# Moving the layer norm's centring from GpSimd to ScalarE in the second attention phase of a four-layer cross-attention kernel

## The chip, the cores and the metric

The kernel runs on one core of one Trainium2 chip. The metric is the device time of one execution in microseconds (us). The engines are named as the profile names them: PE is TensorE, PEld its weight loads, DVE is VectorE, ACT is ScalarE, POOL is GpSimd, SP issues DMAs.

## The reference

Four layers follow each other on x of shape 64 x 128 x 128 (batch, tokens, features), with a context of 77 keys per batch and 16 heads of 8 features. The change is in the second layer, L1, whose end is a residual sum and a layer norm:

```
scores = einsum(q, k) / sqrt(d) * attention_weights
scores = where(attention_mask, -inf, scores)
p_attn = softmax(scores);  out = (p_attn @ v) @ Wo.T + bo
x = queries + out
mu = mean(x, axis=-1);  var = mean(square(x - mu), axis=-1)
return (x - mu) * rsqrt(var + 1e-5) * gamma + beta
```

## The kernel before

The program runs seven phases one after the other: A0, F0, A1, A2, F2, A3, F3. A phases are attention, F phases feed-forward. Only A1 (layer L1) is touched. A phase handles 64 batches in a software pipeline: in step b every engine works on several batches at once, its program being one `step` function per engine in a fixed order, unrolled four times inside a loop. Engines meet only through semaphores, which the code calls events. The tiles of the norm have two slots, used in turn by even and odd batches.

In A1, step b, the engines do this, in this order:

- **DVE** (`step_weighted`): scores times weights for batch b+1 (`weigh`, two halves, L856); `variance(b-3)` (L927, adds epsilon to the variance); `mask(b+1, 0)` (L861, mask tile times a large negative number plus the scores, both in SBUF); `invert` (L896); `peak_masked(b+1, 0)` (L869, row maxima); `normalise`, `keep_v`, `sums(b-2)` (L915); `mask(b+1, 1)` (L861); `statistics(b-2)`; `peak_masked(b+1, 1)` (L869); `aggregate(b-2)` (L923, makes mean and variance).
- **POOL**: `shift(b, 1)` (L989, subtract the row maximum, needs the second peak); `root(b-3)` (L1004, power -1/2 on 128x1); `residual(b-1)` (L995); `centre(b-3)` (L1008, (t - mean) * rstd, 128x128); `shift(b+1, 0)` (L989, needs the first peak of b+1); `affine(b-3)` (L1013 times gamma, L1016 plus beta).
- **ACT**: `keep_att(b-1)` (L799), `keep_oT` (L805), `exps(b, 1)` (L747, needs `shift(b, 1)`), `keep_pT(b, 0)` (L752), `block_keys(b+2)` (four L767), `keep_q` (L786), `keep_xT(b+3)` (L774), `keep_pT(b, 1)` (L752), `exps(b+1, 0)` (L747, needs `shift(b+1, 0)`).
- **PE**: scores of b+1 (L646, needs `block_keys` and `keep_q`), the attention products of b-1 (L681), transposes of the probabilities (L664), the projections (L618 to L707).

`peak_masked(b, k)` also waits until `shift(b-1, k)` has read the maxima, and `sums(b)` until the z of batch b-2 is made. In phases A0 and A2 the POOL program is another branch: `rstd` (L999 adds epsilon on POOL, then `root`), `residual`, `centre`, `block_keys`, `affine`.

Of the kernel before, what the change touches and what calls it, by code (L numbers as in the profile page):

```python
# [138 lines left out]
def build_layers(nc, a, out):  # L139
# [3 lines left out]
    with ExitStack() as ctx:  # L143
# [3 lines left out]
        def slots(name, shape, dt=F32, n=2):  # L147
            return [sb(f"{name}{s}", shape, dt) for s in range(n)]
# [140 lines left out]
        mv_s = slots("mv", [T, 2])  # L289
        var_s = slots("var", [T, 1])  # L290
        rstd_s = slots("rstd", [T, 1])
        z_s = slots("z", [T, D])
        zg_s = slots("zg", [T, D])
        y_s = slots("y", [T, D])
# [77 lines left out]
        def event(name, phases, parts=1, transfers=0):  # L372
            return Event(sem, name, [(ph, NB if ph[0] == "A" else GROUPS) for ph in phases], parts, transfers)
# [37 lines left out]
        mv_made = event("mv_made", CROSS)  # L411
        var_made = event("var_made", CROSS)
        rstd_made = event("rstd_made", CROSS)
        z_made = event("z_made", CROSS)
        zg_made = event("zg_made", CROSS)
        y_made = event("y_made", CROSS)
# [325 lines left out]
        def cross_scalar(act, ph):  # L742
            w = cross[ph]

            def exps(b, k):
                act.wait_ge(shifted.sem(b), shifted.count(ph, b, k))
                nc.scalar.activation(half(p_s[b.par], k), half(p_s[b.par], k), ACT.Exp, scale=SCALE[ph]).then_inc(exp_made.sem(b), 1)  # L747

            def keep_pT(b, k):
                act.wait_ge(pT_made.sem(b), pT_made.count(ph, b, k))  # L750
                wait_earlier(act, att_made, ph, b, 1, k)
                nc.scalar.activation(pT_s[k][:], two[0:C, :], ACT.Copy).then_inc(pT_kept.sem(b), 1)  # L752

            def keep_k(b):
                act.wait_ge(k_made.sem(b), k_made.count(ph, b))
                wait_earlier(act, kblk_made, ph, b, 2)
                src = k_col_bank[:, K_COL:K_COL + C]
                if ph == "A2":
                    nc.scalar.activation(kT_s[b.par][:], src, ACT.Copy).then_inc(k_kept.sem(b), 1)
                else:  # L760
                    nc.scalar.activation(kT_s[b.par][:], src, ACT.Identity, bias=w["bk"][:, 0:1]).then_inc(k_kept.sem(b), 1)

            def block_keys(b):
                act.wait_ge(k_made.sem(b), k_made.count(ph, b))
                wait_earlier(act, s_made, ph, b, 2)
                for h in range(QH):
                    ins = nc.scalar.activation(kblk_s[b.par][:, h * C:(h + 1) * C], k_col_bank[:, K_COL:K_COL + C], ACT.Identity,  # L767
                                               bias=key_bias_rows[:, h:h + 1], scale=rowmask[:, h:h + 1])
                ins.then_inc(kblk_made.sem(b), 1)

            def keep_xT(b):
                act.wait_ge(xT_made.sem(b), xT_made.count(ph, b))
                wait_earlier(act, q_made, ph, b, 2)
                nc.scalar.activation(xT_s[b.par][:], att_bank[:, X_COL:X_COL + T], ACT.Copy).then_inc(xT_kept.sem(b), 1)  # L774

            def keep_q(b, columns):
                act.wait_ge(q_made.sem(b), q_made.count(ph, b))

                if columns:
                    act.wait_ge(xT_made.sem(columns), xT_made.count(ph, columns))  # L780
                wait_earlier(act, s_made, ph, b, 2)
                src = att_bank[:, Q_COL:Q_COL + T]
                if ph == "A2":
                    nc.scalar.activation(qT_s[b.par][:], src, ACT.Copy).then_inc(q_kept.sem(b), 1)
                else:
                    nc.scalar.activation(qT_s[b.par][:], src, ACT.Identity, bias=w["bq"][:, 0:1]).then_inc(q_kept.sem(b), 1)  # L786

            def keep_v(b):
                act.wait_ge(v_made.sem(b), v_made.count(ph, b))
                wait_earlier(act, att_made, ph, b, 2, 1)  # L790
                dst = v_s[b.par][:].rearrange("p (h v) -> p h v", v=VPAIR // 2)[:, :, 0:DH]
                src = v_bank[0:C, V_COL:V_COL + D].rearrange("p (h v) -> p h v", v=DH)
                nc.scalar.activation(dst, src, ACT.Copy).then_inc(v_kept.sem(b), 1)

            def keep_att(b):
                act.wait_ge(att_made.sem(b), att_made.count(ph, b, 1))

                wait_earlier(act, back_made, ph, b, 2)
                nc.scalar.activation(att_s[b.par][:], att_bank[:, 0:2 * T], ACT.Copy).then_inc(att_kept.sem(b), 1)  # L799

            def keep_oT(b):
                act.wait_ge(oT_made.sem(b), oT_made.count(ph, b))
                if (b + -2).exists:
                    act.wait_ge(proj_made.sem(b + -2), proj_made.count(ph, b + -2))
                nc.scalar.activation(oT_s[b.par][:], out_bank[:, OT_COL:OT_COL + T], ACT.Copy).then_inc(oT_kept.sem(b), 1)  # L805

            def step(b, has):
                weighted = ph == "A1"
                if has(-1):
                    keep_att(b + -1)  # L810
                if has(-2) and ph != "A0":
                    keep_oT(b + -2)
                if has(0) and weighted:
                    exps(b, 1)
                if has(0):
                    keep_pT(b, 0)
                if has(2):
                    block_keys(b + 2) if weighted else keep_k(b + 2)
                if has(1) and not weighted:
                    keep_v(b + 1)  # L820
                if has(2):
                    keep_q(b + 2, b + 3 if has(3) else None)
                if has(3):
                    keep_xT(b + 3)
                if has(1) and not weighted:
                    exps(b + 1, 0)
                if has(0):
                    keep_pT(b, 1)
                if has(1):
                    exps(b + 1, 0 if weighted else 1)  # L830
            drive(act, NB, step, reach=REACH)

        def cross_vector(dve, ph):
# [88 lines left out]
            def aggregate(b):  # L922
                nc.vector.bn_aggr(mv_s[b.par][:], stats_s[b.par][:]).then_inc(mv_made.sem(b), 1)  # L923

            def variance(b):
                dve.wait_ge(mv_made.sem(b), mv_made.count(ph, b))
                nc.vector.tensor_scalar(var_s[b.par][:], mv_s[b.par][:, 1:2], LN_EPS, None, ALU.add).then_inc(var_made.sem(b), 1)  # L927

            def step_weighted(b, has):
                if has(1):  # L930
                    weigh(b + 1, 0)
                    weigh(b + 1, 1)
                if has(-3):
                    variance(b + -3)
                if has(1):
                    mask(b + 1, 0)
                if has(-1):
                    invert(b + -1)
                if has(1):
                    peak_masked(b + 1, 0)  # L940
                if has(-1):
                    normalise(b + -1)
                if has(1):
                    keep_v(b + 1)
                if has(-2):
                    sums(b + -2)
                if has(1):
                    mask(b + 1, 1)
                if has(-2):
                    statistics(b + -2)  # L950
                if has(1):
                    peak_masked(b + 1, 1)
                if has(-2):
                    aggregate(b + -2)
# [23 lines left out]
        def cross_gpsimd(pool, ph):  # L978
# [18 lines left out]
            def rstd(b):  # L997
                pool.wait_ge(mv_made.sem(b), mv_made.count(ph, b))
                nc.gpsimd.tensor_tensor(var_s[b.par][:], mv_s[b.par][:, 1:2], ln_eps[:, 0:1], ALU.add).then_inc(var_made.sem(b), 1)  # L999
                root(b)  # L1000

            def root(b):
                pool.wait_ge(var_made.sem(b), var_made.count(ph, b))
                nc.gpsimd.tensor_tensor(rstd_s[b.par][:], var_s[b.par][:], minus_half[:, 0:1], ALU.pow).then_inc(rstd_made.sem(b), 1)  # L1004
                pool.wait_ge(rstd_made.sem(b), rstd_made.count(ph, b))

            def centre(b):
                nc.gpsimd.tensor_scalar(z_s[b.par][:], t_s[b.par][:], mv_s[b.par][:, 0:1], rstd_s[b.par][:, 0:1],  # L1008
                                        ALU.subtract, ALU.mult).then_inc(z_made.sem(b), 1)

            def affine(b):
                pool.wait_ge(z_made.sem(b), z_made.count(ph, b))
# [5 lines left out]
            def step(b, has):  # L1018
                weighted = ph == "A1"
                if weighted:  # L1020
                    if has(0):
                        shift(b, 1)
                    if has(-3):
                        root(b + -3)
                    if has(-1):
                        residual(b + -1)
                    if has(-3):
                        centre(b + -3)
                    if has(1):
                        shift(b + 1, 0)  # L1030
                    if has(-3):
# [1006 lines left out]
```

## Time and profile before

| | us |
|---|---|
| median of 3 runs | 2476.26 |
| range of the runs | 2475.57 to 2477.04 |
| the profiled execution's own time | 2477.04 |
| its span in the trace | 2475.2 |

Over the whole span the profile has PE busy 93%, DVE 76%, POOL 63%, ACT 60%; A1 lies between about 523 and 930 us. Starts in the trace are in us from the span's start; a row's second number is its duration, and what stands in brackets at its end is how long the engine was idle before it and who ended that. Consecutive instructions of one engine overlap by some hundredths of a microsecond in these rows. A duration includes time in which an issued instruction is held up inside its engine.

### The profile page before, as it was taken

What the parts mean: (1) busy time and instruction counts of PE and PEld (TensorE: products, weight loads), DVE (VectorE), ACT (ScalarE), POOL (GpSimd) and SP (SyncE); (2) the same over time, 40 slices, a digit from 0 to 9 for tenths busy, and PEclk for the clock granted to TensorE, in tenths of its full rate; (3) what the DMA queues carried; (4) which work ended last, traced back from release to release, by engine and by line L of the source; (5) the groups of instructions that cost most, each with busy time, mean ns of one, the idle gap of its engine ahead of it and who ended that gap; (6) DMA issues with size and microseconds to landing.
All of it is one profiled execution on the core that took longest, in us unless ns stands there. A gap on an engine that the chain in (4) does not pass through costs nothing.

```text
span 2475.2 us, 83166 instructions
## 1 busy us (share of the span) xinstructions
PE 2305.7 (93%) x26926; PEld 1818.4 (73%) x26926; DVE 1877.8 (76%) x4067; ACT 1476.8 (60%) x3343; POOL 1560.6 (63%) x2374
## 2 busy tenths in 40 slices
PE   6999998988888879999999979999999999999899
PEld 4777777966666667777777867777777777777587
DVE  4777772159999985777775668888888888888566
ACT  4777775558888875888884524444444444444333
POOL 2666663139999992666666766666666666666332
PEclk9999999989999997999999989999999999999999
DMA  4111111245555541222221223333333333333111
GB/s 125 43 43 42 43 41 57 69 134 165 169 166 169 166 116 40 52 51 52 50 48 56 70 71 96 92 96 97 96 95 94 94 94 94 94 94 92 48 56 55
DMA packets 443043, 211.78 MB, mean 86 GB/s; under 512 B 206400, under 2 KB 433856, under 8 KB 442816
## 3 DMA queue, kind: packets, MB, share of 16 engines
q1 hardware_dynamic: 442944, 210.51, 32.1%
q8 instruction: 56, 0.92, 0.2%
q14 instruction: 43, 0.35, 0.0%
HBM read 113.36 MB, written 29.88 MB: 58 GB/s over the span
## 4 chain that ended last, share of the span: by engine, by line
PE 64%; POOL 13%; issue 8%; SPq 5%; ACT 4%; DVE 3%; DMA 2%; POOLq 0%; DVEq 0%; ACTq 0%
PE bank L664 10%; PE bank L1429 8%; PE bank L1389 8%; PE bank L681 5%; PE bank L1126 5%; PE bank L646 4%; PE bank L1457 4%; POOL sb_region L989 4%; PE bank L1140 4%; ACT sb_pT L752 3%; PE bank L1439 3%; PE bank L1415 3%; POOL sb_rstd L1004 2%; SPq L1334 2%; POOL sb_z L1008 2%
## 5 line engine op out<-in xcount | busy, mean ns | idle before, releaser
L664 PE MATMUL bank<-sb_ident,sb_region 128*77 128x128 f32 x3072 | 413.1, 278 | 54.1 <-ACT sb_pT L752 50.5
L752 ACT ACTIVATE sb_pT<-bank 77x1024 f32<-77x1024 f32 x384 | 392.2, 1021 | 82.7 <-PE bank L664 81.9
L664 PEld LDWEIGHTS bank<-sb_ident,sb_region 128*77 128x77 f32 x3072 | 350.0, 151 | 108.2 <-issue 104.3
L1519 ACT ACTIVATE sb_l<-sb_l 128x640 f32<-128x640 f32 x128 | 94.4, 738 | 384.3 <-DVE sb_l L1567 384.3
L843 DVE TENSOR_REDUCE sb_max<-bank 128x8 f32<-128x616 f32 x256 | 203.1, 793 | 149.0 <-PE bank L646 80.4
L747 ACT ACTIVATE sb_region<-sb_region 128x616 f32<-128x616 f32 x384 | 276.8, 721 | 22.9 <-POOL sb_region L989 21.5
L1640 POOL TENSOR_TENSOR sb_pn<-sb_l,sb_r_all 128x512 f32<-128x512 f32 x128 | 134.6, 1052 | 231.9 <-DVE sb_r_all L1577 227.8
L1389 PE MATMUL bank<-sb_region,sb_wqkv 128*128 128x128 f32 x2048 | 253.7, 278 | 1.5 <-DVE sb_region L1555 0.8
L1429 PE MATMUL bank<-sb_wvo,sb_region 128*64 128x512 f32 x1024 | 247.9, 605 | 0.0
L1389 PEld LDWEIGHTS bank<-sb_region,sb_wqkv 128*128 128x128 f32 x2048 | 242.1, 194 | 4.1 <-DVE sb_region L1555 1.4
L681 PEld LDWEIGHTS bank<-sb_pT,sb_v 77*32 77x32 f32 x6144 | 155.9, 109 | 82.2 <-issue 73.4
L848 DVE TENSOR_TENSOR sb_region<-bank,sb_max 128x616 f32<-128x616 f32 x256 | 204.5, 799 | 11.8
L681 PE MATMUL bank<-sb_pT,sb_v 77*32 77x128 f32 x6144 | 209.2, 276 | 3.2 <-ACT sb_pT L752 3.2
L1631 POOL TENSOR_TENSOR sb_region<-sb_region 128x512 f32<-128x512 f32 x128 | 162.9, 1273 | 77.1 <-PE bank L1415 63.1
L646 PE MATMUL bank<-sb_region,sb_qT 32*128 32x308 f32 x1536 | 158.5, 482 | 33.9 <-ACT sb_region L767 21.0
L989 POOL TENSOR_TENSOR sb_region<-sb_region,sb_max 128x616 f32<-128x616 f32 x128 | 173.2, 1353 | 22.2 <-DVE sb_max L869 22.2
L1457 PEld LDWEIGHTS bank<-sb_region,sb_pT 128*64 128x64 f32 x2048 | 121.7, 137 | 77.4 <-issue 68.5
L1175 ACT ACTIVATE sb_fh<-bank,sb_L_xattn_ffb 128x256 f32<-128x256 f32 x256 | 109.4, 473 | 112.2 <-PE bank L1126 112.2
L1503 ACT ACTIVATE sb_region<-bank 128x512 f32<-128x512 f32 x256 | 151.3, 593 | 41.4 <-PE bank L1429 31.8
L1555 DVE TENSOR_TENSOR sb_region<-bank,sb_cosT 128x512 f32<-128x512 f32 x256 | 172.5, 674 | 3.5 <-PE bank L1389 3.3
L1555 DVE TENSOR_TENSOR sb_region<-bank,sb_sinT 128x512 f32<-128x512 f32 x256 | 174.0, 680 | 0.0
L1632 POOL TENSOR_TENSOR sb_region<-sb_region 128x512 f32<-128x512 f32 x128 | 166.2, 1299 | 0.0
(182 smaller groups left out, 5485.6 us busy)
## 6 DMA issues: line engine op xcount, KB each, us to landing
sb_region<-in_side SPq DMA_DIRECT2D x64, 616.0 KB, 3.8
sb_pT<-sb_region SPq DMA_DIRECT2D x512, 64.0 KB, 2.1
sb_kF<-sb_region SPq DMA_DIRECT2D x512, 64.0 KB, 2.1
scratch_after_A<-sb_y SPq DMA_DIRECT2D x256, 64.0 KB, 1.7
sb_fx<-scratch_after_A SPq DMA_DIRECT2D x96, 128.0 KB, 2.1
sb_mask<-in_mask SPq DMA_DIRECT2D x64, 154.0 KB, 2.3
sb_x<-scratch_after_F SPq DMA_DIRECT2D x128, 64.0 KB, 1.9
sb_ctx<-in_ctxT SPq DMA_DIRECT2D x192, 38.5 KB, 1.8
```

Source lines behind the costliest of these rows:

```text
L646: mm = nc.tensor.matmul(bank[c][:, 0:QC], qT_s[b.par][rows, :], kblk_s[b.par][rows, :], start=(ph != "A0"), stop=(ph != "A2"))
L664: mm = nc.tensor.transpose(two[0:C, h * T:(h + 1) * T], p_s[b.par][:, head * C:(head + 1) * C], ident[:])
L681: mm = nc.tensor.matmul(att_bank[32 * i:32 * i + 32, k * T:(k + 1) * T], v_s[b.par][:, first:first + 32], pT_s[k][:, h * T:(h + 1) * T], s ...
L747: nc.scalar.activation(half(p_s[b.par], k), half(p_s[b.par], k), ACT.Exp, scale=SCALE[ph]).then_inc(exp_made.sem(b), 1)
L752: nc.scalar.activation(pT_s[k][:], two[0:C, :], ACT.Copy).then_inc(pT_kept.sem(b), 1)
L843: nc.vector.tensor_reduce(dst, by_bank_and_head(scores_half(k)), AX.X, ALU.max).then_inc(max_made.sem(b), 1)
L848: nc.vector.tensor_tensor(by_bank_and_head(by_bank(half(p_s[b.par], k))), by_bank_and_head(scores_half(k)), spread_max(k), ALU.subtract).t ...
L989: nc.gpsimd.tensor_tensor(by_head(half(p_s[b.par], k)), by_head(half(p_s[b.par], k)), spread(max_s[:, 8 * k:8 * k + 8], C), ALU.subtract)\
L1389: mm = nc.tensor.matmul(rope_bank[eo][:, n * T:(n + 1) * T], wqkv[:, col:col + 128], xnT_s[b.lap], start=True, stop=True)
L1429: mm = nc.tensor.matmul(vo_banks[g][r * SEG:(r + 1) * SEG, :], xnT_s[b.lap][:, g * SEG:(g + 1) * SEG], wvo[:, (2 * h + r) * HC * D:(2 * h ...
L1457: nc.tensor.matmul(out3_bank[g * SEG:(g + 1) * SEG, 0:D], pT_s3[h][:, c * T + g * SEG:c * T + (g + 1) * SEG], vo_s[h][:, (g * HC + c) * D: ...
L1555: ins = nc.vector.tensor_tensor(part[what][eo].rearrange("p (n t) -> p n t", t=T), src, table[:].unsqueeze(1).to_broadcast([128, BLOCKS, T ...
```

## The change

In A1 alone, z = (t - mean) * rstd is made by ACT as rstd * t + shift, with shift = -mean * rstd made by POOL as a 128x1 column. POOL's 128x128 `centre` goes. DVE's `variance` goes, and POOL adds epsilon itself as it does in the other attention phases, so that three 128x1 operations stand on POOL: add, power, product. The new ACT `centre` stands after `keep_xT(b+3)` and ahead of `keep_pT(b, 1)`. Two waits are new besides those of the data: ACT waits until POOL has read the z of batch b-5, and POOL until ACT has made it. A0 and A2 issue what they did.

```diff
+            def centre(b):                                  # cross_scalar
+                act.wait_ge(mean_scaled.sem(b), mean_scaled.count(ph, b))
+                wait_earlier(act, zg_made, ph, b, 2)
+                nc.scalar.activation(z_s[b.par][:], t_s[b.par][:], ACT.Identity, bias=shift_s[b.par][:, 0:1], scale=rstd_s[b.par][:, 0:1])\
+                    .then_inc(z_made.sem(b), 1)
...
                 if has(3):
                     keep_xT(b + 3)
+                if has(-3) and weighted:
+                    centre(b + -3)
...
-            def variance(b):                                # cross_vector
-                dve.wait_ge(mv_made.sem(b), mv_made.count(ph, b))
-                nc.vector.tensor_scalar(var_s[b.par][:], mv_s[b.par][:, 1:2], LN_EPS, None, ALU.add).then_inc(var_made.sem(b), 1)
...
-                if has(-3):
-                    variance(b + -3)
...
+            def scale_mean(b):                              # cross_gpsimd
+                nc.gpsimd.tensor_scalar(shift_s[b.par][:], mv_s[b.par][:, 0:1], rstd_s[b.par][:, 0:1], -1.0, ALU.mult, ALU.mult)\
+                    .then_inc(mean_scaled.sem(b), 1)
...
                     if has(-3):
-                        root(b + -3)
+                        rstd(b + -3)
+                        wait_earlier(pool, z_made, ph, b + -3, 2)
                     if has(-1):
                         residual(b + -1)
                     if has(-3):
-                        centre(b + -3)
+                        scale_mean(b + -3)
                     if has(1):
                         shift(b + 1, 0)
```

## Rows read from the trace of the kernel before

**Rows 1.** Busy time of each engine in the steady part of A1.
```profile
565.00:900.00 335.00, 283.26 (x3724) 225.94 (x3725) 314.34 (x708) 290.16 (x653) 316.97 (x383) 1.00 0.56 166
```

**Rows 2.** Timeline of DVE and POOL, one step of A1.
```profile
700.28 0.80 DVE L869 TENSOR_REDUCE sb_max<-sb_region 128x8 f32<-128x616 f32 x1
...
701.30 1.50 DVE L856 TENSOR_TENSOR sb_region<-bank,sb_region 128x616 f32<-128x616 f32 x2
702.03 1.21 POOL L989 TENSOR_TENSOR sb_region<-sb_region,sb_max 128x616 f32<-128x616 f32 x1
702.72 0.14 DVE L927 TENSOR_SCALAR sb_var<-sb_mv 128x1 f32<-128x1 f32 x1
702.78 1.12 DVE L861 SCALAR_TENSOR_TENSOR sb_region<-sb_mask,sb_region 128x616 f32<-128x616 uint8 x1
703.21 1.12 POOL L1004 TENSOR_TENSOR sb_rstd<-sb_var,sb_minus_half 128x1 f32<-128x1 f32 x1
...
704.03 0.79 DVE L869 TENSOR_REDUCE sb_max<-sb_region 128x8 f32<-128x616 f32 x1
704.40 0.45 POOL L995 TENSOR_TENSOR sb_xb<-sb_xr,sb_L_xattn_bo 128x128 f32<-128x128 f32 x1
704.84 0.80 POOL L1008 TENSOR_SCALAR sb_z<-sb_t,sb_mv,sb_rstd 128x128 f32<-128x128 f32 x1
...
705.33 0.79 DVE L861 SCALAR_TENSOR_TENSOR sb_region<-sb_mask,sb_region 128x616 f32<-128x616 uint8 x1
705.61 1.58 POOL L989 TENSOR_TENSOR sb_region<-sb_region,sb_max 128x616 f32<-128x616 f32 x1
706.44 0.80 DVE L869 TENSOR_REDUCE sb_max<-sb_region 128x8 f32<-128x616 f32 x1
...
707.69 0.46 POOL L1016 TENSOR_TENSOR sb_y<-sb_zg,sb_L_xattn_ln_b 128x128 f32<-128x128 f32 x1
708.11 1.22 POOL L989 TENSOR_TENSOR sb_region<-sb_region,sb_max 128x616 f32<-128x616 f32 x1
709.08 0.90 DVE L861 SCALAR_TENSOR_TENSOR sb_region<-sb_mask,sb_region 128x616 f32<-128x616 uint8 x1
...
710.62 0.45 POOL L995 TENSOR_TENSOR sb_xb<-sb_xr,sb_L_xattn_bo 128x128 f32<-128x128 f32 x1 [0.23 <-POOL sb_rstd L1004]
```

**Rows 3.** The same timeline at the head of A1.
```profile
545.08 1.22 POOL L989 TENSOR_TENSOR sb_region<-sb_region,sb_max 128x616 f32<-128x616 f32 x1 [1.56 <-DVE sb_max L869]
545.52 1.44 DVE L861 SCALAR_TENSOR_TENSOR sb_region<-sb_mask,sb_region 128x616 f32<-128x616 uint8 x1
548.07 1.22 POOL L989 TENSOR_TENSOR sb_region<-sb_region,sb_max 128x616 f32<-128x616 f32 x1 [1.77 <-DVE sb_max L869]
549.45 0.79 DVE L861 SCALAR_TENSOR_TENSOR sb_region<-sb_mask,sb_region 128x616 f32<-128x616 uint8 x1
549.61 1.05 POOL L1004 TENSOR_TENSOR sb_rstd<-sb_var,sb_minus_half 128x1 f32<-128x1 f32 x1 [0.32 <-DVE sb_var L927]
551.57 0.79 DVE L861 SCALAR_TENSOR_TENSOR sb_region<-sb_mask,sb_region 128x616 f32<-128x616 uint8 x1
551.94 1.50 POOL L989 TENSOR_TENSOR sb_region<-sb_region,sb_max 128x616 f32<-128x616 f32 x1
```

**Rows 4.** POOL's timeline late in A1.
```profile
899.80 1.12 POOL L1004 TENSOR_TENSOR sb_rstd<-sb_var,sb_minus_half 128x1 f32<-128x1 f32 x1
```

**Rows 5.** POOL's timeline in A0, and between F0 and A1.
```profile
124.48 0.19 POOL L999 TENSOR_TENSOR sb_var<-sb_mv,sb_ln_eps 128x1 f32<-128x1 f32 x1 [1.51 <-DVE sb_mv L923]
124.75 0.56 POOL L1004 TENSOR_TENSOR sb_rstd<-sb_var,sb_minus_half 128x1 f32<-128x1 f32 x1
...
515.03 0.18 POOL L1728 TENSOR_SCALAR sb_pool_var<-sb_pool_var 64x1 f32<-64x1 f32 x1 [5.65 <-DVE sb_pool_var L1719]
```

**Rows 6.** ACT's groups, 565 to 900 us: count, busy, mean ns, idle before.
```profile
L767 ACT ACTIVATE sb_region<-bank,sb_key_bias_rows,sb_rowmask 128x77 f32<-128x77 f32 x216 | 70.9, 408 | 0.0
L799 ACT ACTIVATE sb_region<-bank 128x256 f32<-128x256 f32 x55 | 21.2, 385 | 26.2 <-PE bank L681 26.2
```

More of the change, by code:

```diff
@@ L291, in build_layers @@
         rstd_s = slots("rstd", [T, 1])
+        shift_s = slots("mean_shift", [T, 1])
         z_s = slots("z", [T, D])
@@ L413, in build_layers @@
         rstd_made = event("rstd_made", CROSS)
+        mean_scaled = event("mean_scaled", ["A1"])
         z_made = event("z_made", CROSS)
@@ L932, in step_weighted @@
                     weigh(b + 1, 1)
-                if has(-3):
-                    variance(b + -3)
-                if has(1):
                     mask(b + 1, 0)
@@ L999, in rstd @@
                 nc.gpsimd.tensor_tensor(var_s[b.par][:], mv_s[b.par][:, 1:2], ln_eps[:, 0:1], ALU.add).then_inc(var_made.sem(b), 1)
-                root(b)
-            def root(b):
                 pool.wait_ge(var_made.sem(b), var_made.count(ph, b))
```

## The prediction

> **What bounds the kernel now.** I read the page's slices first, to see that the changed phase A1 is some 400 of 2475 us; then the busy times of its steady part; then the timeline of POOL and DVE step by step. The busy times say that POOL is the fullest engine: 316.97 of 335 us, DVE 314.34, ACT 290.16 [rows 1]. The pace is (899.80 - 549.61) / 57 = 6.14 us per step between the first and the last of 58 L1004 rows [rows 3, 4].
>
> The timeline says why POOL is full, and that is what the prediction rests on. Three 128x1 or 128x616 POOL operations take longer here than their work. L1004 takes 0.56 us in A0 and 1.12 here [rows 2, 5]. L989 takes 1.22 us in one place and 1.58 in another [rows 2]. Each long one has a DVE mask (L861) running at its start, and what is left after that mask's end is always the same: L1004 ends 704.33, the mask ended 703.90, so 0.43 later; L989 ends 707.19, the mask ended 706.12, so 1.07; at the head of A1 551.94 + 1.50 - (551.57 + 0.79) = 1.08, and 549.61 + 1.05 - 550.24 = 0.42 [rows 2, 3]. It works the other way round too: the mask takes 0.79 alone, but 1.12 when it starts at 702.78 while L989 runs until 703.24 (its end is 0.66 behind that), and 1.44 when it starts at 545.52 behind an L989 that ends 546.30 (again 0.66) [rows 2, 3]. So a mask and a POOL operation on two SBUF tiles never run together: who asks first goes, the other is held. L1008, one tile with two columns, runs 704.84 to 705.64 beside the mask of 705.33, and neither is longer [rows 2].
>
> In the steady state POOL is late. The second mask (705.33) comes 0.28 us ahead of `shift(b+1, 0)` (705.61), and at the head of A1 0.37 ahead (551.57, 551.94) [rows 2, 3]. That order closes a ring through both engines: first mask's end 703.90, second mask's start +1.43, its end +0.79, L989's end +1.07, L1013, L1016 and the next L989 up to 709.33 (+2.14), the next first mask's end 709.98 (+0.65). The sum is 6.08 [rows 2]. L1004, L995 and L1008 are not on it: L989 issued at 705.61 could not run before 706.12 anyway.
>
> **What the change removes and adds.**
>
> POOL loses L1008: 0.80 us [rows 2]. It gains L999 (0.19, and L1004 starts 0.27 after L999 does [rows 5]) and the product, for which L1728, the same kind of operation on 64x1, has 0.18 [rows 5]; with column operands I take 0.18 and bound it by 0.18 and 0.45, the residual's whole 128x128. The wait on z costs POOL a decode at most; the gap behind L1004 is 0.07 in one place and 0.22 in another with the same waits [rows 2], so 0 to 0.15. Counting from the first mask's end M: before, L1004 ended M+0.43, L995 ran M+0.50 to M+0.95, L989 stood at M+1.71. After: L999 ends M+0.05 (what is left of it once the mask releases it, as 0.43 is left of 0.56), L1004 runs M+0.13 to M+0.69, L995 starts M+0.76 or M+0.91, the product ends M+1.38 or M+1.53, and L989 stands at M+1.35 or M+1.50. So POOL is 0.2 to 0.35 us earlier at this point.
>
> The second mask stands at M+1.43. It used to win by 0.28; now it is a dead heat, and in the places with the short gap L989 is 0.08 ahead. At the head of A1 it is clearer: L1004 no longer waits 0.32 for DVE's L927 [rows 3]. L989 (548.07) ends 549.29, L999 is done 549.44, the mask (0.06 earlier without L927, 549.39) ends 550.18, L1004 550.60, L995 about 551.12 to 551.27, L989 starts 551.26 to 551.41, the mask at 551.51. POOL goes first from there.
>
> **What happens once POOL is first.** It stays first, because it now waits for DVE's peaks instead of for the mask. One step, from the second mask's end: second peak's end +1.12 (706.12 to 707.24 [rows 2]); L989 starts +0.08 (548.07 behind a peak; POOL was idle) and runs +1.22; L999, gap and L1004 +0.79 (-0.04+0.19+0.08+0.56); the first mask, asking meanwhile, ends +0.66 behind L1004; the first peak's end +0.92 (703.90 to 704.82 [rows 2]); L989 +0.07 and +1.22; the second mask, which would have started 0.51 after that peak, is held and ends +0.66. Sum 6.74 us. POOL's L995 and product fit between: L995, held by the mask, ends M+0.31, the product M+0.48, the peak M+0.92. If the first mask asks before L1004 (it starts 0.22 + 1.42 after the peak's end [rows 2], L1004 0.08 + 1.22 + 0.23 after it: 1.64 against 1.53), the sum is 1.12 + 0.22 + 1.42 + 0.79, then L1004 0.42, L995 and product 0.84, L989 1.22, mask 0.66, which is 6.69. Either way about 6.7, 0.6 slower.
>
> DVE loses L927, 0.06 us of start distance (702.72, 702.78 [rows 2]); it is in neither sum above except as 1.42 for 1.48. ACT gains a 128x128 activation with two column operands: L767 has 0.408 for 77 columns and two such operands [rows 6], so I take 0.45, bounds 0.41 and 0.68 (scaled by columns). ACT waits 26.2 us over 55 steps, 0.48 each, for PE's L681 right after this place [rows 6]; that covers it, less the 0.1 by which rows overlap. Behind it in ACT's queue stand `keep_pT(b, 1)` and `exps(b+1, 0)`; they have the same 0.48. Without that cover it would cost 64 x 0.35 = 22 us. z is made while POOL runs L989, so L1013 waits at most some hundredths, inside the slack ahead of the second peak. SP's queue is not touched.
>
> The Trainium skill has a rule that speaks against this change ("SBUF — State Buffer", "SBUF: two separate sides"): the pair of ports that DVE shares with GpSimd is an exclusive lock, taken by whoever starts first, for the whole instruction. By that rule L1004 keeps the mask out for all of its run, as in the 6.74. Its wording covers any GpSimd operation that reads SBUF; the trace does not bear that out for L1008 [rows 2].
>
> Sum: some 59 of the 64 steps have both masks and a norm on POOL, 59 x (6.74 - 6.14) = 35 us. Against the profiled execution 2477.04 + 35 = 2512; that execution lies 0.8 above the median, so 2511 beside the runs shown.
>
> **The rivals.**
>
> - *L1004 does not keep the mask out* (no row has a mask starting inside it; its bounds are 0 and 0.42). Then the first mask runs 1.42 behind the peak: 1.12 + 0.22 + 1.42 + 0.79 + 0.92 + 0.07 + 1.22 + 0.66 = 6.42, +16 us, 2493. Chance 0.12.
> - *POOL first in part of the steps only*, if the order falls back in some of the four unrolled places: between 2477 and 2508. Chance 0.07.
> - *The second mask still goes first.* The ring of 6.08 is then intact, and POOL's gain is lost in L989's hold; DVE's 0.06 in the steps where it counts gives 0 to 4 us: 2472 to 2476. It needs POOL's extras to reach 0.1 to 0.25 more than I take. Chance 0.12.
> - *Faster: POOL's queue is what counts.* Then a step loses 0.80 and gains 0.05 + 0.08 + 0.13 (the whole 0.56 in place of 0.43) + 0.18 = 0.44: 5.78, and DVE's own queue without holds allows that (1.43 + 0.79 + 1.12 + 0.22 + 1.42 + 0.79 = 5.77). 60 x 0.36 = 22 us, 2455. It decides if masks and L989 stop meeting, but L989 is ready 0.07 behind the first peak and runs 1.22, the mask asks 0.51 behind it. Chance 0.07. The Trainium skill's advice to relieve the most-contended engine first ("Perfetto Trace Analysis", "Identifying the Most-Contended Engine") would give this; the held L989 speaks against it.
>
> **How the numbers follow.** The forecast has 0.62: 2511, on its own 2500 to 2520 (gaps of 0.15 either way on 59 steps). The range of 0.8 leaves out the faster and the unchanged case (0.19): 2480 to 2520. No change means within 0.2% (5 us), about what a measurement can tell. Slower: 0.62 + 0.12 + 0.07 = 0.81; same 0.12; faster 0.07.
>
> **What would show it.** In A1, the second L861 of a step at about 1.4 us instead of 0.79, L989 down to 1.22 everywhere and idle before it waiting for L869, L1004 back at 0.56, L861's first at 1.0 or more, a pace of 6.7. ACT's new row near 0.45, its wait for L681 no shorter than before. Wrong, if L989 ahead of L1013 still takes 1.4 to 1.6: then the pace is 6.1; or if L1004 runs at 0.56 with a mask of 0.79 inside it: then 6.4.

## The result and the profile after

| | before | after |
|---|---|---|
| median of 5 runs each, same chip | 2476.26 us | 2492.00 us |
| range | 2471.88 to 2478.22 | 2488.88 to 2493.47 |
| the profiled execution's own time, its span | 2477.04, 2475.2 | 2491.23, 2489.5 |

The ratio is 1.0063, with a 95% interval from 1.0051 to 1.0075. The kernel is 15.7 us slower. The prediction was slower by 35 us (2511, range 2480 to 2520). The direction came true and the time lies in the range, but 35 us were forecast and 15.7 came, and by another mechanism than the one forecast.

Two words are used from here on. An operation is held when it has been issued but makes no progress until an operation of the other engine is done; its row is then longer than its work. Its lead is how much earlier it is issued than the operation of the other engine that it meets.

In the changed kernel the lines are: DVE mask L871, `weigh` L866, peak L879; POOL `shift` L992, epsilon L1002, power L1004, residual L998, product L1013, gamma L1018, beta L1021; ACT's centre L800, `exps` L749, `keep_pT` L754.

The busy times of the steady part, in the columns of [rows 1] (the page's order PE, PEld, DVE, ACT, POOL):

```profile
565.00:900.00 335.00, 280.77 (x3608) 216.09 (x3607) 315.01 (x639) 301.82 (x690) 311.82 (x424) 1.00 0.55 162
```

DVE and POOL are still the fullest, both at 93 to 94%, and POOL is busy 5 us less, where 55 operations of 0.80 us are gone. The pace is the distance of the L1004 rows. Taken from the 6th to the 57th of the 64, it went from 6.149 us per step before to 6.324 after.

The timeline of DVE and POOL at the head of A1, which answers to [rows 3]:

```profile
548.85 0.19 POOL L1002 TENSOR_TENSOR sb_var<-sb_mv,sb_ln_eps 128x1 f32<-128x1 f32 x1
548.99 0.79 DVE L871 SCALAR_TENSOR_TENSOR sb_region<-sb_mask,sb_region 128x616 f32<-128x616 uint8 x1
549.12 1.08 POOL L1004 TENSOR_TENSOR sb_rstd<-sb_var,sb_minus_half 128x1 f32<-128x1 f32 x1
550.71 0.26 POOL L1013 TENSOR_SCALAR sb_mean_shift<-sb_mv,sb_rstd 128x1 f32<-128x1 f32 x1
550.93 1.22 POOL L992 TENSOR_TENSOR sb_region<-sb_region,sb_max 128x616 f32<-128x616 f32 x1
551.12 1.68 DVE L871 SCALAR_TENSOR_TENSOR sb_region<-sb_mask,sb_region 128x616 f32<-128x616 uint8 x1
```

Here POOL's L992 is 0.19 us ahead of the second mask, runs its full 1.22, and the mask is held: 1.68 instead of 0.79. That is the order the prediction said. It lasts for three steps, those ahead of the loop. The same timeline where the loop begins, and one step of the steady part, which answers to [rows 2]:

```profile
569.64 0.27 POOL L1013 TENSOR_SCALAR sb_mean_shift<-sb_mv,sb_rstd 128x1 f32<-128x1 f32 x1
569.87 1.90 POOL L992 TENSOR_TENSOR sb_region<-sb_region,sb_max 128x616 f32<-128x616 f32 x1
569.91 0.79 DVE L871 SCALAR_TENSOR_TENSOR sb_region<-sb_mask,sb_region 128x616 f32<-128x616 uint8 x1
...
699.94 1.29 DVE L871 SCALAR_TENSOR_TENSOR sb_region<-sb_mask,sb_region 128x616 f32<-128x616 uint8 x1
700.53 0.75 POOL L1002 TENSOR_TENSOR sb_var<-sb_mv,sb_ln_eps 128x1 f32<-128x1 f32 x1
701.36 0.55 POOL L1004 TENSOR_TENSOR sb_rstd<-sb_var,sb_minus_half 128x1 f32<-128x1 f32 x1
702.21 0.45 POOL L998 TENSOR_TENSOR sb_xb<-sb_xr,sb_L_xattn_bo 128x128 f32<-128x128 f32 x1 [0.30 <-POOL sb_rstd L1004]
702.64 0.94 POOL L1013 TENSOR_SCALAR sb_mean_shift<-sb_mv,sb_rstd 128x1 f32<-128x1 f32 x1
702.66 0.79 DVE L871 SCALAR_TENSOR_TENSOR sb_region<-sb_mask,sb_region 128x616 f32<-128x616 uint8 x1
703.54 1.21 POOL L992 TENSOR_TENSOR sb_region<-sb_region,sb_max 128x616 f32<-128x616 f32 x1
704.72 0.45 POOL L1018 TENSOR_TENSOR sb_zg<-sb_z,sb_L_xattn_ln_g 128x128 f32<-128x128 f32 x1
705.34 0.46 POOL L1021 TENSOR_TENSOR sb_y<-sb_zg,sb_L_xattn_ln_b 128x128 f32<-128x128 f32 x1 [0.17 <-POOL sb_zg L1018]
705.75 1.22 POOL L992 TENSOR_TENSOR sb_region<-sb_region,sb_max 128x616 f32<-128x616 f32 x1
706.20 1.42 DVE L871 SCALAR_TENSOR_TENSOR sb_region<-sb_mask,sb_region 128x616 f32<-128x616 uint8 x1
```

At 569.87 L992 is only 0.04 ahead of the mask, and the mask goes first all the same: it keeps its 0.79 and L992 takes 1.90, until 1.07 behind the mask's end. The lead has gone from 0.19 to 0.04 because the residual L998 starts 0.33 behind the end of the power there (568.89, 569.22), against 0.07 at the head (550.20, 550.27), while the mask comes only 0.09 later. From there on the order is the old one. In every steady step the second mask has its 0.79, and what meets it is now the product. It takes 0.26 alone (550.71) and 0.94 here; its end, 703.58, is 0.13 behind the mask's (703.45). Over 57 places between 545 and 905 us the border is sharp: issued 0.27 us or more ahead of the mask it takes 0.26 or 0.27 (5 places), issued 0.24 ahead to 0.01 behind it takes 0.91 to 1.08 (52 places).

The same step of the kernel before (both are the 25th of A1 that has a norm; [rows 2] shows the end of this step and the whole of the next, another of the four unrolled places) has its first mask's end at 697.74, and then:

```profile
699.17 0.79 DVE L861 SCALAR_TENSOR_TENSOR sb_region<-sb_mask,sb_region 128x616 f32<-128x616 uint8 x1
699.60 1.44 POOL L989 TENSOR_TENSOR sb_region<-sb_region,sb_max 128x616 f32<-128x616 f32 x1
701.61 0.46 POOL L1016 TENSOR_TENSOR sb_y<-sb_zg,sb_L_xattn_ln_b 128x128 f32<-128x128 f32 x1 [0.17 <-POOL sb_zg L1013]
```

So the ring is still closed, with one link exchanged. From the first mask's end (701.23) to the second mask's start it is 1.43, as before; to that mask's end 0.79, as before. Then L992 is no longer held itself. It starts behind the held product, at 703.54, and ends 1.30 behind the mask's end, where L989 ended 1.08 behind it (701.04 against 699.96). From there to the end of the next L992 it is 2.22 (706.97), was 2.20; to the next first mask's end 0.65 (707.62), was 0.66. The sum is 6.39; before it was 6.16 in this step. The exchanged link alone makes 0.22 of the 0.23 us. The four unrolled places take 6.39, 6.23, 6.29 and 6.41 in turn, where they took 6.16, 6.08, 6.15 and 6.24.

How this adds up over the kernel: the L1004 rows stand 10.3 us later at the 60th (pace, 59 x 0.175 = 10.3) and 10.7 at the last (938.92 against 928.22). Then comes the tail of A1. ACT's timeline there:

```profile
937.13 0.49 ACT L800 ACTIVATE sb_z<-sb_t,sb_mean_shift,sb_rstd 128x128 f32<-128x128 f32 x1 [1.07 <-POOL sb_mean_shift L1013]
939.87 0.49 ACT L800 ACTIVATE sb_z<-sb_t,sb_mean_shift,sb_rstd 128x128 f32<-128x128 f32 x1 [2.24 <-POOL sb_mean_shift L1013]
940.26 0.20 ACT L1795 ACTIVATE sb_poolT<-bank 128x64 f32<-128x64 f32 x1
```

and PE's:

```profile
940.52 0.69 PE L1742 MATMUL bank<-sb_poolT,sb_wmem 128*128 128x64 f32 x2 [3.31 <-ACT sb_poolT L1795]
```

The copy L1795, which the next phase's preparation needs, stands in ACT's queue behind the last centre, and that waits for POOL's last product. Before, the same copy ran 1.2 us ahead of POOL's last power and PE waited 0.31 for it. PE's L1742 is 13.25 us later than its counterpart of before (940.52 against 927.27), so the tail costs 2.5; PE makes up 2.4 of it in the weight products that follow. A2 starts 10.9 us later (958.92 against 948.07). The last power of A2 is 11.0 later and the end of the span 14.3, so the 3.3 us between them, and 1.4 more up to the 15.7 between the medians, arise behind A2 or lie in the spread, where the code is unchanged. Executions of one kernel spread by 5 to 7 us in most sets and by 11 in one, so I put no cause to them.

### The profile page after: what moved, and what is told of

Its sections match the earlier page's. It is cut to its first block, busy times and chain, and to the rows that moved or that the text cites. A ratio compares the mean times of both kernels' runs of the same rounds, so it can differ in the third digit from the quotient of the medians.

```text
span 2489.5 us, 83367 instructions
## 1 busy us (share of the span) xinstructions
PE 2309.8 (93%) x26926; PEld 1812.6 (73%) x26926; DVE 1890.8 (76%) x4003; ACT 1498.7 (60%) x3407; POOL 1559.8 (63%) x2438
## 4 chain that ended last, share of the span: by engine, by line
PE 62%; POOL 15%; issue 7%; SPq 7%; ACT 3%; DVE 3%; DMA 1%; POOLq 1%; DVEq 0%; ACTq 0%
PE bank L666 10%; PE bank L1435 8%; PE bank L1395 8%; POOL sb_region L992 5%; PE bank L1132 5%; PE bank L683 5%; PE bank L648 4%; PE bank L1146 4%; PE bank L1463 4%; ACT sb_pT L754 3%; PE bank L1445 2%; PE bank L1421 2%; SPq L1337 2%; SPq L1340 2%; POOL sb_mean_shift L1013 2%
## 5 line engine op out<-in xcount | busy, mean ns | idle before, releaser
L754 ACT ACTIVATE sb_pT<-bank 77x1024 f32<-77x1024 f32 x384 | 391.6, 1020 | 81.5 <-PE bank L666 80.5
L749 ACT ACTIVATE sb_region<-sb_region 128x616 f32<-128x616 f32 x384 | 277.0, 722 | 25.4 <-POOL sb_region L992 25.4
L683 PE MATMUL bank<-sb_pT,sb_v 77*32 77x128 f32 x6144 | 216.2, 277 | 3.8 <-ACT sb_pT L754 3.6
L1637 POOL TENSOR_TENSOR sb_region<-sb_region 128x512 f32<-128x512 f32 x128 | 162.5, 1270 | 77.5 <-PE bank L1421 63.3
L1002 POOL TENSOR_TENSOR sb_var<-sb_mv,sb_ln_eps 128x1 f32<-128x1 f32 x192 | 68.0, 354 | 172.2 <-DVE sb_mv L933 172.2
L992 POOL TENSOR_TENSOR sb_region<-sb_region,sb_max 128x616 f32<-128x616 f32 x128 | 158.9, 1241 | 22.3 <-DVE sb_max L879 22.3
```

Source lines behind the costliest of these rows:

```text
L683: mm = nc.tensor.matmul(att_bank[32 * i:32 * i + 32, k * T:(k + 1) * T], v_s[b.par][:, first:first + 32], pT_s[k][:, h * T:(h + 1) * T], s ...
L992: nc.gpsimd.tensor_tensor(by_head(half(p_s[b.par], k)), by_head(half(p_s[b.par], k)), spread(max_s[:, 8 * k:8 * k + 8], C), ALU.subtract)\
```

## The experiments

Theory at the start: DVE's masks and POOL's two-tile operations exclude each other, and this alone sets the pace in both kernels. First rival: ACT's new activation costs time in ACT's own queue. Second rival: the new chain power, product, ACT's z, gamma costs time. (In the trace of the changed kernel, POOL's gamma waits 0.5 us in all for z between 565 and 900 us, which speaks against the second.) Times are medians; each ratio is to the kernel before, run on the same chip (2478.0, 2478.6 and 2478.1 us in the three sets). Pace is from the 6th to the 57th power.

**Masks that read PSUM, in the kernel before.** `weigh` writes its product back to PSUM and the mask takes one operand from there, so it has one SBUF input. The wait for the SBUF half moves with it from `weigh` to the mask, and PE may write the bank again only after the mask and not after `weigh`.

```diff
-                nc.vector.tensor_tensor(by_bank(half(p_s[b.par], k)), scores_half(k), ...side..., ALU.mult)
+                nc.vector.tensor_tensor(scores_half(k), scores_half(k), ...side..., ALU.mult)
...
-                nc.vector.scalar_tensor_tensor(half(p_s[b.par], k), half(mask_s[b.par], k), MASKED, half(p_s[b.par], k),
+                nc.vector.scalar_tensor_tensor(..p_s.., ..mask_s.., MASKED, scores_half(k),
```

> The kernel before, but in A1 the weighted scores stay in their PSUM banks and the mask reads them there (one SBUF input in place of two), so that no DVE instruction of A1 reads two SBUF tiles. Theory (masks and POOL operations hold each other): every L861 back at 0.79 us, every L989 at 1.22, L1004 at 0.56, pace of A1 5.8 us per step in place of 6.14, time 20 us lower, 2455. Rival (POOL's queue length sets the pace, holds are a symptom): POOL's own work is 5.31 us per step, so the pace falls as well, but masks or L989 keep long rows. Rival (ACT and PE set the pace): L989 and masks shorten, the pace stays 6.1, no change in time.

2454.81 us, ratio 0.9907 [0.9892, 0.9922], pace 5.737. Its timeline around the second mask of one step (L861 is the mask, L989 the shift):

```profile
701.04 0.78 DVE L861 SCALAR_TENSOR_TENSOR sb_region<-sb_mask,bank 128x616 f32<-128x616 uint8 x1
...
704.47 0.79 DVE L861 SCALAR_TENSOR_TENSOR sb_region<-sb_mask,bank 128x616 f32<-128x616 uint8 x1
```

```profile
703.03 1.22 POOL L989 TENSOR_TENSOR sb_region<-sb_region,sb_max 128x616 f32<-128x616 f32 x1
704.64 0.56 POOL L1004 TENSOR_TENSOR sb_rstd<-sb_var,sb_minus_half 128x1 f32<-128x1 f32 x1 [0.40 <-DVE sb_var L927]
```

L1004 is issued 0.17 behind a mask and takes its 0.56, where [rows 2] had 1.12, and the mask of 701.04 runs beside L989 (700.90 to 702.12) with both at their plain durations. So the exclusion was worth 23 us in the kernel before, net of the two waits that moved, and it does not act on a mask with one SBUF input. The Trainium skill states just this condition ("SBUF — State Buffer", "SBUF: two separate sides"): a DVE operation with two SBUF inputs takes the port pair only against a GpSimd operation that reads SBUF. This run agrees: with one SBUF input the mask takes 0.78 beside a shift of 1.22, issued 0.14 ahead of it.

**A spare ACT activation in the kernel before**, of the same shape, at the centre's place, with nothing behind it.

```diff
+                nc.scalar.activation(spare_s[b.par][:], ident[:], ACT.Identity, bias=ident[:, 0:1], scale=ident[:, 1:2])
```

> The kernel before with one more ACT activation of 128x128 with two column operands in every step of A1, at the place of the new centre; nobody uses its result. Theory (the loss is the held product and the later L989): the 0.5 us lies in ACT's wait for L681 (0.48 per step), time 0 to 2 us up. Rival (the loss is ACT's longer queue): the whole 16 us of the change appear, 2492.

2479.03, ratio 1.0007 [0.9998, 1.0016], pace 6.165. The spare takes 503 ns on average, as the real centre does. ACT's wait ahead of `keep_att` falls from 0.48 to 0.22 a step. The prediction's cover for ACT's work holds at this pace; the first rival is worth 1 us here.

**Epsilon on POOL in the kernel before**; the centre stays on POOL.

```diff
-                    variance(b + -3)        # DVE
...
-                        root(b + -3)        # POOL
+                        rstd(b + -3)
```

> Only the part of the change that moves epsilon: DVE's L927 goes, POOL does L999 in A1 too, and keeps its 128x128 centre (no work on ACT). POOL's centre is then issued 1.2 to 1.4 us behind the first mask's end, 0 to 0.2 ahead of the second mask. Theory (a one-tile operation issued that close is held as the product is): the centre takes 1.4 to 1.6 us, the pace rises to 6.7 to 6.9, 35 to 45 us slower. If a one-tile operation of this size is not held: L989 still waits for the mask's end as before, no change. Rival (ACT's queue): no change.

2522.64, ratio 1.0183 [1.0168, 1.0199], pace 6.909. Moving 0.14 us from DVE to POOL costs 45 us:

```profile
704.71 1.53 POOL L1002 TENSOR_SCALAR sb_z<-sb_t,sb_mv,sb_rstd 128x128 f32<-128x128 f32 x1
704.78 0.79 DVE L861 SCALAR_TENSOR_TENSOR sb_region<-sb_mask,sb_region 128x616 f32<-128x616 uint8 x1
706.22 1.21 POOL L983 TENSOR_TENSOR sb_region<-sb_region,sb_max 128x616 f32<-128x616 f32 x1
```

The centre (L1002 here, one tile and two columns), issued 0.07 ahead of the mask, is held to 0.67 behind the mask's end, and the shift L983 starts 0.65 behind that end instead of being in the air. In this trace the centre takes 1.52 to 1.60 at every lead from 0.06 to 0.31. In [rows 2] the same centre is 0.49 ahead of the mask and takes 0.80, and so it does, in this run and in the kernel before with and without the spare activation, at every lead of 0.33 or more, with the mask beside it at its plain 0.79. So a mask does hold one-tile operations; they only look immune when they are issued early enough. This is the mistake that the prediction made about the product. That they hold a mask in turn was not seen in any trace.

**The changed kernel with DVE's variance kept** (POOL has the power and the product only).

> The changed kernel with DVE's variance kept (POOL has the power and the product only, ACT the centre). POOL's power ends 0.42 behind the first mask, the product is over before the second mask, and L989 is ready 0 to 0.3 us ahead of it. Theory: the product is back at 0.26 us; where L989 leads by 0.2 or more it goes first and the second mask takes 1.5 to 1.7 us, pace 6.4 to 6.7, 2490 to 2510; in the steps where it leads by less the mask goes first and the step is that of before. Rival (ACT's queue): 2492 again, with the second mask at 0.79.

2485.24, ratio 1.0026 [1.0016, 1.0035], pace 6.209: 7 us below the changed kernel by the times, 9 by the ratios, and 5 below the 2490 to 2510 expected. The order is mixed. POOL's rows, two steps, with the masks (L871) that meet the shift L999:

```profile
701.83 1.97 POOL L999 TENSOR_TENSOR sb_region<-sb_region,sb_max 128x616 f32<-128x616 f32 x1
...
707.59 0.26 POOL L1021 TENSOR_SCALAR sb_mean_shift<-sb_mv,sb_rstd 128x1 f32<-128x1 f32 x1
707.81 1.21 POOL L999 TENSOR_TENSOR sb_region<-sb_region,sb_max 128x616 f32<-128x616 f32 x1
```

```profile
701.94 0.78 DVE L871 SCALAR_TENSOR_TENSOR sb_region<-sb_mask,sb_region 128x616 f32<-128x616 uint8 x1
...
708.11 1.57 DVE L871 SCALAR_TENSOR_TENSOR sb_region<-sb_mask,sb_region 128x616 f32<-128x616 uint8 x1
```

L999 is 0.11 ahead in one step and loses (1.97), 0.30 ahead in the next and wins (mask 1.57). The product is free (0.26) in both. With 0.27 less on POOL, the product has moved out of the mask's reach and the shift into it. Over the four unrolled places the shift's leads are 0.04, 0.12, 0.29 and 0.14, and it wins only the 0.29; the gaps behind the power there are 0.33, 0.30, 0.08 and 0.22.

**The changed kernel without the product.** ACT's bias is the unscaled mean, so the scaling of the mean is left out.

```diff
-                        scale_mean(b + -3)
...
-                ... bias=shift_s[b.par][:, 0:1], scale=rstd_s...
+                ... bias=mv_s[b.par][:, 0:1], scale=rstd_s...
```

> The changed kernel without POOL's product: ACT's centre takes the unscaled mean as its bias, so z is another value; that part of the computation is left out. POOL's L992 is then issued 1.2, 1.35 or 1.45 us behind the first mask's end, 0.25 ahead of the second mask or behind it. Theory: in the places where it leads by 0.15 or less it is held and ends 1.07 behind the mask as in the kernel before; where it leads by 0.19 or more it goes first and the mask takes 1.6. Pace 6.15 to 6.3, 2477 to 2487, below the changed kernel. Rival (ACT's queue or the added waits): 2492, as the changed kernel.

2487.41, ratio 1.0033 [1.0021, 1.0044], pace 6.245. Here POOL is first in every steady step (the shift leads by 0.28 to 0.43), the order that the prediction was made for, without the product. DVE's and POOL's rows (shift L992):

```profile
702.10 1.57 DVE L871 SCALAR_TENSOR_TENSOR sb_region<-sb_mask,sb_region 128x616 f32<-128x616 uint8 x1
703.99 0.80 DVE L879 TENSOR_REDUCE sb_max<-sb_region 128x8 f32<-128x616 f32 x1
704.79 1.47 DVE L866 TENSOR_TENSOR sb_region<-bank,sb_region 128x616 f32<-128x616 f32 x2
706.18 0.79 DVE L871 SCALAR_TENSOR_TENSOR sb_region<-sb_mask,sb_region 128x616 f32<-128x616 uint8 x1
707.09 0.80 DVE L879 TENSOR_REDUCE sb_max<-sb_region 128x8 f32<-128x616 f32 x1
708.39 1.44 DVE L871 SCALAR_TENSOR_TENSOR sb_region<-sb_mask,sb_region 128x616 f32<-128x616 uint8 x1
```

```profile
704.86 1.22 POOL L992 TENSOR_TENSOR sb_region<-sb_region,sb_max 128x616 f32<-128x616 f32 x1 [0.26 <-DVE sb_max L879]
706.31 1.07 POOL L1004 TENSOR_TENSOR sb_rstd<-sb_var,sb_minus_half 128x1 f32<-128x1 f32 x1
707.96 1.22 POOL L992 TENSOR_TENSOR sb_region<-sb_region,sb_max 128x616 f32<-128x616 f32 x1
```

The step, from the second mask's end (703.67): peak's end +1.12; first mask's start +1.39 (706.18) and end +0.79; first peak's end +0.92; L992 +0.07 and +1.22; second mask's end +0.65. The sum is 6.16, against my 6.74 or 6.69. The first mask asks 0.13 ahead of the power and so waits for nothing; and `weigh` starts at once behind the peak, without the 0.22 of [rows 2] that I had carried over (there a step waits 0.27 for PE's scores, at 707.60; with DVE later they are ready).

**The product on DVE**, behind the second mask, in the changed kernel.

> The changed kernel with the product on DVE, right behind the second mask. Theory: POOL as without the product; DVE has 0.07 to 0.2 more between the second mask and the second peak, which is beside the held L989 and so mostly hidden; 2478 to 2492, below the changed kernel or equal to it. Rival: 2492 and more.

2525.48, ratio 1.0183 [1.0163, 1.0203], pace 6.84, missed by 33 us. POOL is first in every steady step (second masks 1.44 to 1.63), and the product behind the held mask comes late for ACT:

```profile
706.87 0.50 ACT L800 ACTIVATE sb_z<-sb_t,sb_mean_shift,sb_rstd 128x128 f32<-128x128 f32 x1 [0.71 <-DVE sb_mean_shift L937]
```

POOL waits 68.6 us over 48 steps for this z. The ring is: z, gamma, beta, shift, the norm's operations, shift, held mask, product, z. A small operation put behind the held one ties both holds into one chain; I had priced only its 0.2 us.

**Two spare powers** behind the power in the changed kernel, a single execution.

```diff
+                nc.gpsimd.tensor_tensor(spare_s[b.par][:, k:k + 1], var_s[b.par][:], minus_half[:, 0:1], ALU.pow)   # k = 0, 1
```

> The changed kernel with two more powers of 128x1 on POOL behind L1004 in every step of A1 (results unused), so that second masks start inside a power. If a power keeps a mask out for all of its run, those masks take 0.9 to 1.2 us and end 0.66 behind the power; if not, they take 0.79 and the power is 0.56 or is held itself. Time: 15 to 50 us above the changed kernel either way.

2550.97. It shows the one case that no row had, a mask that starts inside a power (the two spares are one row, x2):

```profile
608.14 1.49 POOL L1022 TENSOR_TENSOR sb_spare<-sb_var,sb_minus_half 128x1 f32<-128x1 f32 x2 [0.24 <-POOL sb_rstd L1006]
```

```profile
608.43 0.79 DVE L873 SCALAR_TENSOR_TENSOR sb_region<-sb_mask,sb_region 128x616 f32<-128x616 uint8 x1
```

The mask starts 0.29 into the first spare and keeps its 0.79. The second spare is held and ends 0.41 behind the mask. Eight such places between 600 and 660 us (0.29 to 0.59 behind the first spare's start) have masks of 0.79. The price that my first rival named, the power not keeping the mask out, is thus right from 0.29 us on; in the changed kernel no mask starts there, so it was not what decided.

**PSUM masks in the changed kernel**, both edits together.

> The changed kernel with the masks reading the scores from PSUM, as in e1, so that no mask holds a POOL operation. Theory (the change loses only by meeting the masks): the loss is gone; beside e1 (2454.8) the step loses DVE's 0.06 and the phase's end costs some 3 us for the last centres in ACT's queue: 2452 to 2458, the product 0.26 us everywhere, L992 1.22. Rival (the added ACT work or the longer chain of waits costs as such): 10 us or more above e1.

2468.51, ratio 0.9962 [0.9948, 0.9975], pace 5.947: a miss. All holds are gone (masks 0.78, product 0.26, shift 1.22), and yet it is 13.7 us above the kernel before with the same masks. Over 330 us POOL waits 32.3 for ACT's z. Its rows of ACT and POOL:

```profile
704.89 0.72 ACT L749 ACTIVATE sb_region<-sb_region 128x616 f32<-128x616 f32 x1
705.52 1.00 ACT L754 ACTIVATE sb_pT<-bank 77x1024 f32<-77x1024 f32 x1
706.42 1.31 ACT L769 ACTIVATE sb_region<-bank,sb_key_bias_rows,sb_rowmask 128x77 f32<-128x77 f32 x4
...
708.03 0.50 ACT L800 ACTIVATE sb_z<-sb_t,sb_mean_shift,sb_rstd 128x128 f32<-128x128 f32 x1
```

```profile
702.70 0.46 POOL L1018 TENSOR_TENSOR sb_zg<-sb_z,sb_L_xattn_ln_g 128x128 f32<-128x128 f32 x1 [0.64 <-ACT sb_z L800]
703.65 1.21 POOL L992 TENSOR_TENSOR sb_region<-sb_region,sb_max 128x616 f32<-128x616 f32 x1
...
708.60 0.46 POOL L1018 TENSOR_TENSOR sb_zg<-sb_z,sb_L_xattn_ln_g 128x128 f32<-128x128 f32 x1 [0.55 <-ACT sb_z L800]
```

This is a ring that the change itself makes (the second rival, once the holds are gone): gamma waits for z (702.70), beta, `shift(b, 1)` to 704.86, `exps(b, 1)` on ACT starts 0.03 later, then `keep_pT`, `block_keys`, `keep_q`, `keep_xT` and the centre, which ends 708.53, and gamma again at 708.60. The round is 5.90. Two more runs are to tell it from ACT's load alone.

**PSUM masks and the spare activation, in the kernel before.**

> The kernel before with the masks reading PSUM (2454.8 us) and a spare ACT activation of 128x128 with two column operands ahead of keep_pT(b, 1); nothing depends on it and nothing else of the change is in it. Theory: with the holds gone ACT and PE are the ring that sets the pace, and the 0.50 us put ahead of keep_pT(b, 1) delays PE's second L681; most of the 13.7 us by which the changed kernel with PSUM masks lies above 2454.8 is this: pace 5.85 to 5.95 (5.74 without), 2461 to 2467 us. Rival: the 13.7 us come from the longer chain power, product, ACT's z, POOL's gamma, which is absent here: pace 5.74, 2453 to 2457.

2458.13, ratio 0.9919 [0.9906, 0.9933], pace 5.837. ACT's 0.50 us without the dependency costs 3.3 us by the medians, between the two expectations. The profiled execution, from which the pace is, was the slowest of its five (2463.78), 8.2 above the profiled one with PSUM masks alone (2455.55). So ACT's load has 3 to 8 of the 13.7 us, and what is left, 4 to 10, belongs to the rest of the change, the ring through z and the tail together; the runs don't divide it more closely.

**PSUM masks in the changed kernel, the centre moved behind `keep_pT(b, 1)`.**

> The changed kernel with the masks reading PSUM (2468.5 us) and ACT's centre moved behind keep_pT(b, 1), ahead of exps(b+1, 0). Theory (ACT's queue ahead of keep_pT(b, 1)): PE's second L683 gets its input 0.4 earlier and the pace falls to 5.75 to 5.85, if z comes early enough: 2456 to 2463. Rival (the chain to z): z is made 0.6 to 1.0 later, POOL, which already waits 0.6 for it, waits longer, and the pace stays or rises: 2468 to 2485.

2525.40, ratio 1.0191 [1.0177, 1.0205], pace 6.90. The round through z has become longer by `keep_pT`'s 1.03 less the overlap of 0.10, 5.95 + 0.93 = 6.88. That is the rival's sign, and 40 us more than its 2485, since I had expected part of the delay to be covered; on the ring that sets the pace nothing is. So z is on that ring in the run with PSUM masks.

**The changed kernel with the centre moved in the same way**, masks in SBUF.

> The changed kernel with ACT's centre moved behind keep_pT(b, 1), masks as they were (in SBUF). Theory (ring over DVE's masks and POOL's L992): z stands off the ring while L992 covers it, and L992 takes 1.21 behind the second mask; z is made 0.6 to 1.0 later than it is, of which about 0.5 is covered, so POOL's gamma comes 0.1 to 0.5 later: 2492 to 2515. Rival (ACT's queue ahead of keep_pT(b, 1) sets the pace in the changed kernel too): 2480 to 2488.

2545.13, ratio 1.0272 [1.0256, 1.0287], pace 7.18: 30 us above the upper end of what was expected. I take it that the same ring of 6.88 takes over here too (POOL waits 1.41 for z in a step that I read), and that what the masks still hold comes on top; the 0.30 between 6.88 and 7.18 was not taken apart. In the changed kernel as it stands this ring, at about 5.95, is covered by the 6.32 of masks and shifts.

## Why the prediction was right or wrong

M is the first mask's end, as in the prediction.

- *Masks and two-tile POOL operations never run together, and the ring through them sets the pace.* Right: masks with one SBUF input, which hold nothing, gave 23 us (2454.81), which was also the time of my rival "faster" (2455), reached by another way.
- *POOL stands at M+1.35 to M+1.50 with L989.* Too early. L1002 ends M+0.05 and L1004 M+0.68, as worked out. But the gap behind L1004 is 0.08, 0.22, 0.30 or 0.32 by place, and the product takes 0.26, not 0.18. The product starts at M+1.19, 1.33, 1.41 and 1.44; free of holds, the shift would follow 0.23 later (550.71 to 550.93), at M+1.42, 1.56, 1.64 and 1.67, against the mask's M+1.43: 0.01 ahead in one place and behind in three. The M+1.71 of before was also the earliest of four places; the other three have M+1.85. The rival "the second mask still goes first" had said that 0.1 to 0.25 more on POOL would do this.
- *POOL stays first.* This is the step that failed. It was first from the head of A1, as forecast, and lost its place at the loop's entry, where the longer gap behind the power left it a lead of only 0.04. The prediction took it that who asks first goes, and the rule that it cites says the same. It is not enough to ask first: in this place (the mask behind `sums`, the shift behind the product) every shift ahead by 0.15 us or less was held, 45 in three traces, and every one ahead by 0.19 or more went first. With the loop's gaps POOL could not have stayed first: a shift that is first stands at M+1.15 with a gap of 0.08 (550.93), so at some 1.29, 1.37 and 1.39 with the others (an estimate), a lead of 0.14, 0.06 and 0.04. The run with DVE's variance kept bears this out: 0.14, 0.12 and 0.04, and the shift loses in these three places.
- *The step with POOL first takes 6.74.* This term was mis-sized too: the steps at the head take 6.23 to 6.24, and the run without a product, where POOL stays first, has 6.245. The two mistakes are those named at that run: the power keeping the first mask out, and the 0.22 ahead of `weigh`. With the head's step the forecast for this order would have been some 59 x 0.09 = 5 us. With the loop's gaps and the product it would have been more: from the second mask's end to the next M 3.30 (run without a product), then the shift at M+1.15 to 1.39, 1.22 and 0.65, in the mean 6.47, which is some 19 us (an estimate). Either is well under 35.
- *With the second mask first, the ring of 6.08 stays whole* (the rival of 2472 to 2476). The order came true, its price did not. The product was taken as free beside the mask, like L1008 in [rows 2]. It is held for the mask's length, so that L992, which used to have only 1.07 of its time left at the mask's end, starts 0.09 behind that end and takes its whole 1.21. That is 0.22 of the 0.23 us in the step shown. The pace rose by 0.175 a step, 10.3 us over 59 steps. No run takes this hold away and leaves the rest as it is (without the product the order changes as well), so its share rests on these rows.
- *Slower.* The direction was right, but by luck: a step made longer by masks held behind shifts was forecast, and what came was a held product in front of the shift, in an order for which the prediction had said 0 to 4 us faster.
- *ACT's centre is covered.* Right at this pace (2479.03 with a spare one), with 0.50 us instead of 0.45. Not seen at all was the round z, gamma, beta, shift, `exps`, centre of 5.95; it costs next to nothing while masks and shifts hold the pace at 6.32 (gamma waits 0.5 us in all), and 4 to 10 us, the tail with it, once they don't. Nor was the tail: the last centre holds back the copy L1795, 2.5 us, nearly all regained by PE before A2.

What stays open: the 3 to 5 us that arise behind A2 with unchanged code; why the gap behind the power differs from place to place, which decides where POOL loses its place and was read from the traces only; and why a shift with the smaller lead loses.

## What to carry to other kernels

When two engines exclude each other, price the operation that stands at the meeting point and not only the one that is moved: a 0.26 us column product in front of a shift cost more than the hold it kept the shift out of. Here small operations paid the whole hold if they were issued in the last 0.24 us (the product) or 0.31 us (the centre) ahead of the mask. Removing the exclusion (one operand in PSUM) brought 23 us; every way of moving work between the engines, with the masks left in SBUF, cost 7 to 67. And an operation handed to a third engine makes a new round through that engine's queue: write that round out, with all that stands ahead of it in the queue, before calling it covered.

## What the runs showed of the hardware

- POOL operations on 128x1 and 128x128 with column operands are held by a DVE mask with two SBUF inputs, like two-tile ones. The product: 0.26 alone, 0.91 to 1.08 when issued up to 0.24 us ahead of the mask; 0.27 when issued 0.27 ahead. The centre on POOL: 0.80 alone or at a lead of 0.33 or more, 1.52 to 1.60 at 0.06 to 0.31. Unlike two-tile operations, the centre did not hold the mask that started inside it (0.79).
- An operation can be held by a mask that starts later, at the second mask up to 0.15 us later for the shift (1.90 at a lead of 0.04, 1.97 at 0.11); at a lead of 0.19 it is the mask that is held. At the first mask, behind `weigh` and with the shift behind beta, 0.01 to 0.06 was lead enough: with epsilon on POOL a shift 0.03 ahead took 1.22 and the mask 1.84. What makes the two places differ isn't settled.
- What a held operation still has to do behind the mask's end: the shift 1.07, whether it was issued ahead of the mask or behind it, the power 0.41 to 0.43, the product 0.13 (issued together) or 0.05 (issued 0.24 ahead).
- A power of 0.55 us does not hold a mask that starts 0.29 us or more behind it, while a 128x128 or 128x616 operation on two tiles does, to 0.65 behind its own end (in the same trace a mask 0.07 behind beta took 1.04).
- An ACT Identity of 128x128 with column scale and bias takes 0.50 us, where the plain 128x128 copy takes 0.28; the one reads SBUF and the other PSUM, which was not varied.
